# Macaron block: the two copies of the values between partition halves issued by ScalarE behind its last copy of the values, not by SyncE

## The reference, cut to what matters

```python
x = L0_attn_x                                   # (8, 512, 128)
x = x + 0.5 * ffn(layernorm(x), ...)            # DEPTH = 2 layers inside
x = x + attention(layernorm(x), ...)
x = x + 0.5 * ffn(layernorm(x), ...)
```

```python
h = shift_token(x)
q, k, v = split(h @ wqkv)                       # 8 heads of 64
q, k = rotary_xpos(l2norm(q) * qs, l2norm(k) * ksc)
o = local_attention(q, k, v)                    # 64 queries see their own 64 keys and the 64 before
x = x + o @ wo
h = layernorm(shift_token(x)) * lg + lb
a, g = split(h @ w1 + b1)
x = x + (a * gelu(g)) @ w2 + b2
```

## Time and profile before

| | |
|---|---|
| median of 3 runs | 2125.99 us (2122.33 to 2130.37) |
| profiled execution: time | 2119.46 us |
| profiled execution: span of its instructions | 2117.6 us |
| TensorE matmul busy | 1765.7 us (83%) |
| VectorE busy | 1332.1 us (63%) |
| GpSimd busy | 982.2 us (46%) |
| ScalarE busy | 945.8 us (45%) |
| feed-forward phases in the span | about 84 to 830 us and 1340 to 2110 us |

### The profile page before, as it was taken

How to read it: one execution, slowest core, us unless ns; L and a number is a source line. 1 busy time by engine, 2 the same in 40 slices (tenths; PEclk the granted TensorE clock), 3 DMA queues, 4 the chain that set the end, 5 groups by cost and what they waited for, 6 DMA issues and landing times. The chain is left out here.

```text
span 2117.6 us, 48273 instructions
## 1 busy us (share of the span) xinstructions
PE 1765.7 (83%) x19914; PEld 1023.4 (48%) x19914; DVE 1332.1 (63%) x2002; ACT 945.8 (45%) x1503; POOL 982.2 (46%) x692
## 2 busy tenths in 40 slices
PE   1578888899988887799999996678888998988886
PEld 1244445555545454455555553344545555555543
DVE  2567777666776663466666664577766676666763
ACT  1234444545455443255555554234444454544542
POOL 2444544455454451544444441444445555545540
PEclk9789999999999999599999998789999999999998
DMA  4334434454444551000000000243444534455541
GB/s 145 38 59 69 71 67 64 78 78 83 69 74 71 78 87 33 12 1 1 1 2 1 2 1 1 38 74 64 65 78 72 87 64 69 73 84 82 93 75 41
DMA packets 66060, 118.94 MB, mean 56 GB/s; under 512 B 13183, under 2 KB 23603, under 8 KB 63667
## 3 DMA queue, kind: packets, MB, share of 16 engines
q1 hardware_dynamic: 65843, 115.85, 32.6%
HBM read 49.61 MB, written 3.28 MB: 25 GB/s over the span
## 5 line engine op out<-in xcount | busy, mean ns | idle before, releaser
L953 POOL TENSOR_TENSOR QK<-QK,RB 128x1024 f32<-128x1024 f32 x128 | 302.6, 2365 | 438.7 <-DMA RB<-RN 438.4
L793 DVE SCALAR_TENSOR_TENSOR TP<-banks,cols,tab 128x1024 f32<-128x1024 f32 x256 | 321.1, 1276 | 89.7 <-PE banks L457 73.6
L947 POOL TENSOR_TENSOR QK<-TP 128x512 f32<-128x512 f32 x128 | 164.6, 1286 | 275.8 <-DVE TP L793 199.3
L1315 DVE TENSOR_REDUCE NM<-banks 128x2 f32<-128x1024 f32 (+3 forms) x256 | 202.9, 820 | 126.4 <-PE banks L1128 126.3
L1244 ACT ACTIVATE PTL<-banks 128x1024 f32<-128x1024 f32 (+1 forms) x192 | 167.9, 883 | 189.0 <-PE banks L1159 186.4
L649 ACT ACTIVATE SQ<-banks 128x512 f32<-128x512 f32 x128 | 76.5, 597 | 281.1 <-PE banks L457 281.1
L816 DVE TRANSPOSE_TENSOR_REDUCE MX<-banks 128x16 f32<-128x512 f32 x256 | 160.4, 683 | 60.1 <-PE banks L494 60.1
L834 DVE TENSOR_TENSOR OT<-banks,OT 128x512 f32<-128x512 f32 x128 | 85.3, 688 | 163.2 <-DMA OT<-sums_d 146.4
L457 PE MATMUL banks<-HTH,wqkv_h 128*128 128x512 f32 x256 | 128.8, 503 | 58.4 <-POOL HTL L939 33.3
L948 POOL TENSOR_TENSOR QK<-TP 128x512 f32<-128x512 f32 x128 | 165.1, 1290 | 0.0
L677 ACT ACTIVATE PT<-banks 128x512 f32<-128x512 f32 x256 | 132.2, 603 | 49.8 <-PE banks L508 49.8
(11 more groups left out here) (182 smaller groups left out, 3667.3 us busy)
## 6 DMA issues: line engine op xcount, KB each, us to landing
RB<-RN SPq DMA_DIRECT2D x512, 64.0 KB, 4.0
OT<-sums_d SPq DMA_DIRECT2D x128, 256.0 KB, 4.0
V<-V SPq DMA_DIRECT2D x32, 512.0 KB, 6.1
V<-V SPq DMA_DIRECT2D x32, 384.0 KB, 7.1
RB<-vars_d SPq DMA_DIRECT2D x32, 256.0 KB, 3.3
X<-in_L_attn_x SPq DMA_DIRECT2D x8, 256.0 KB, 4.5
out<-X SPq DMA_DIRECT2D x8, 256.0 KB, 4.7
wqkv_raw<-in_L_ffn_wqkv SPq DMA_DIRECT2D x1, 1536.0 KB
```

What stands on the lines that cost most here:

```text
L793: nc.vector.scalar_tensor_tensor(out=TP[:, o:o + 2, :], in0=BK[4 + z][:, :].unsqueeze(1).to_broadcast([P, 2, T]), scalar=q, in1=tab[:, e, ...
L947: nc.gpsimd.tensor_tensor(QK[:, m, 0, :], TP[:, 2, :], TP[:, 1, :], ALU.subtract)
L953: nc.gpsimd.tensor_tensor(QK[:, m, :, :], QK[:, m, :, :], RB[:, m, :].unsqueeze(1).to_broadcast([P, 2, T]), ALU.mult).then_inc(S["nr_ok"], 1)
L1315: last = nc.vector.tensor_reduce(NM[:, G % 2, i, 24 + 32 * h0:57 + 32 * h0:32], PAIR[at(m) % RING][:, :, o:o + (i + 1) * P], AX_X, ALU.max ...
```

## The change

SyncE's task `values` is removed. ScalarE's task `values`, after the last of its four copies (t = 3), waits until all four are complete and then issues the same two DMAs on its own queue.

```diff
-                        def values(u):
-                            sp.wait_ge(S["ve_ok"], 4 * (u + 1))
-                            sp.dma_start(V1[0:W, :, :], V0[0:W, :, :]).then_inc(S["v1_ok"], 16)
-                            sp.dma_start(V1[W:P, 1:NT, :], V0[W:P, 0:NT - 1, :]).then_inc(S["v1_ok"], 16)
-
...
                             run(norms, n - 1)
                             run(result, n - 4)
-                            run(values, n - 1)
                             run(variances, n - 2)
...
                             nc.scalar.activation(V0[:, t, :], BK[k][:, :], ACT.Copy).then_inc(S["ve_ok"], 1)
+                            if t == NT - 1:
+                                act.wait_ge(S["ve_ok"], 4 * (u + 1))
+                                act.dma_start(V1[0:W, :, :], V0[0:W, :, :]).then_inc(S["v1_ok"], 16)
+                                act.dma_start(V1[W:P, 1:NT, :], V0[W:P, 0:NT - 1, :]).then_inc(S["v1_ok"], 16)
```

## The result

The changed kernel takes 2276.25 us (median of 4 runs, 2270.51 to 2293.06), the kernel before 2128.06 us beside it. The ratio is 1.0721, 95% interval 1.0686 to 1.0757: 7.2% or 148 us slower. The direction was forecast, the size was not: 2276 lies above the range, which ended at 2232.

A forecast was written before the change was run, and what follows sets the result against it. Bound by the path from piece 2's `RB` loads through GpSimd and VectorE to TensorE; 2.5 us delay less 0.5 slack, 28 x 2.0 = 56 us, on 2126 gives 2182 us, 2.6% slower; range 2130 to 2232.

The forecast's parts named there:

- SyncE's two issues cost nothing: On SyncE, removing a wait and two issues (0.86 + 0.81 us) gains nothing, hidden in the 11.7 us wait for `RV`.
- ScalarE's issues cost nothing: On ScalarE after its last copy, the two issues (1.7 us) fit in the 5.16 us it stands waiting for TensorE.
- Piece 0 and piece 1 stay on time: GpSimd's products of the first two pieces: only the tail of their loads can meet the copies; given no delay.
- The path: `RB` of piece 2, GpSimd, VectorE, TensorE, with half a microsecond of slack: Late `RB` loads of piece 2 delay GpSimd's product and `rotate`, then VectorE and TensorE; slack 0.5 us before `rotate`.
- The delay of piece 2, 2.5 us, bounds 1.33 and 3.66: In the DMA engines, V copies delay the last `RB` load of piece 2 by 1.33 to 3.66 us; middle 2.5 taken.
- "heavier" rival: SyncE's issues held, whole transfer first, piece 1 late: 104 us, 2230; with TensorE's clock dip up to 2265; chance 0.14.
- The length of a unit, 44 us: One unit of the loop was taken as 44 us before the change and some 46 us after it.
- The loss per unit is delay less slack, with the clock left to the rival: Per unit 2.5 us delay less 0.5 slack leaves 2.0 us; TensorE's clock dip, up to 1.7 us, left out.

The follow-up runs named there:

- With seven: The changed kernel with the same bytes issued by ScalarE at the same moment as seven DMAs of 64 rows of 2 KB instead of two: 2198.02 us, ratio 1.0344.
- the swap: The changed kernel with GpSimd's `rotate` of the next unit before the product of piece 2: 2141.65 us; the same on the kernel before, as control: 2132.05 us.
- the padded version: The changed kernel with V1's tiles 32 B apart, so the same two DMAs have rows of 2 KB: 2268.48 us, ratio 1.0655.
- the filler: The changed kernel with 28 more transposes on TensorE in the hole, in 28 units: 2230.87 us, ratio 1.0522.
- half of the bytes: The kernel before with only the second copy (384 KB) issued early by ScalarE, the first staying on SyncE: 2217.27 us, ratio 1.0419.

## Why the prediction was right in sign and wrong in size

- *SyncE's two issues cost nothing.* Right. The hole before `RV` is still there: in the unit shown the issues end at 568.47 and `RV` goes at 581.35.
- *ScalarE's issues cost nothing.* Right for two issues: the squares' wait of 4.95 us is ended by TensorE. With seven it is wrong, as the rows show.
- *Piece 0 and piece 1 stay on time.* Right: the product of piece 1 and the scores of g = 0 did not move (10.19 and 10.24, 12.78 and 12.71 in the same averages).
- *The path: `RB` of piece 2, GpSimd, VectorE, TensorE, with half a microsecond of slack.* Right, shown by the swap. The slack was larger: GpSimd's idle time before `rotate` is 0.81 us in the mean of 28 units of the kernel before, 0.85 by the table, where three units had given 0.5.
- *The delay of piece 2, 2.5 us, bounds 1.33 and 3.66.* This step failed; it is 4.65. First the upper bound was too low: it came from 251 GB/s, a rate read in two microseconds in the middle of a transfer, while the whole takes 4.5 to 5 us. The trace of before had the better row: the second copy was issued at 431.94 and landed 6.6 us later or more, 4.1 us or more behind the last `RB` load. Second, I took a place inside the bounds because I thought that rows of the two queues alternate. They do not take such turns: a load issued behind a V copy lands as a rule with it or later (0.12 us later in the median of the padded version), and SyncE's next two issues are held for 2.24 and 3.10 us. The "heavier" rival named this mechanism, and the clock with it, and gave it 0.14. It too had a step wrong, that piece 1 would be late, and its upper end of 2265 lies below the 2276 measured.
- *The length of a unit, 44 us.* That was one unit; the mean of the 28 is 45.95 us, and it grew to 51.29. No term of the sum hung on it.
- *The loss per unit is delay less slack, with the clock left to the rival.* This step failed too. I had seen the fall behind the hole of before, priced it at 1.7 us and kept it out of the sum without a reason. It followed from my own forecast: a hole of 2 us was what I predicted for TensorE. It cost 1.9 us in front of the scores, of which the filler won back up to 1.4 us of the unit; and it cost nearly as much with half of the bytes as with all.

Put together as the runs had it: 4.65 - 0.85 + 2.1 - 0.56 = 5.34 us a unit. With the delay right and the clock left out, the sum would have been 28 x 3.8 = 106 us, 2232, the very edge of the range.

The version with late copies from ScalarE equals the kernel before (0.9982, interval across 1). None of these versions beats the kernel before; the place of the copies behind the `RB` loads was already free.

## What to carry to other kernels

A DMA moved to another engine's queue to "start early" also loses its place behind the loads that matter more. Look for what is in flight at the new moment, take its DMA share, and if that is 1.00 count the whole time that the moved transfer takes alone (4.6 us here) as the delay of the load behind it. If large transfers must go beside urgent small ones, issue them in smaller pieces, on an engine that can afford to be held; here seven pieces instead of two halved the loss (3.4% against 7.2%) and did not remove it. Once a wait opens on TensorE, price the work behind it at half clock if that work is on the path: behind one hole it was, behind the other it was not.

## What was not expected of the hardware

- Two engines that issue DMAs at the same time do so in step, one DMA each: starts 0.00 to 0.01 us apart in four consecutive pairs, each 1.13 to 1.52 us long where one alone takes 0.6. But an issuer that is alone is held too: behind two large copies of its own, SyncE's next two issues took 2.57 and 2.58 us.
- A load issued behind a large copy on the other queue landed 0.12 us after that copy in the median (56 pairs, the padded version).
- Cutting the rows of a transfer from 8 and 6 KB to 2 KB changed its effect on the other queue little (4.65 to 4.02 us), cutting it into seven DMAs much (to 1.56 us).
- An empty stretch of 3.6 us on TensorE was followed by 10 us at 0.51 of the clock in a stretch that TensorE was busy 86%; the same stretch with filler work ran at 1.00.
